# Layer 2, VectorE: the low part of the next batch's first query is made ahead of the statistics of the finished batch

## What is computed

```python
xn = layernorm(x)                          # layer 2's input
a  = layernorm(xn) * g1
q  = l2norm(a @ Wq.T)  * 4                 # 16 heads of 64
k  = l2norm(a @ Wk.T)  * 4;  v = a @ Wv.T  # one head
p  = softmax(causal(q @ k.T))
att = layernorm((p @ v) @ Wout.T) * g2
ffn = (silu(xn @ Wgate.T) * (xn @ Wup.T)) @ Wdown.T
out = x + att + ffn
```

## Time and profile before

| what | value |
|---|---|
| median of 3 runs | 1303.96 us (1302.86 to 1304.91) |
| the profiled execution's own time | 1300.34 us |
| its span, first to last instruction | 1298.5 us |
| mean granted clock of TensorE | 0.964 of full speed |
| busy: PE, DVE, ACT, POOL | 1168.2, 892.5, 669.9, 466.3 us |
| instructions | 27029 |

### The profile page before, as it was taken

How to read it: one execution, slowest core, us unless ns; L and a number is a source line. 1 busy time by engine, 2 the same in 40 slices (tenths; PEclk the granted TensorE clock), 3 DMA queues, 4 the chain that set the end, 5 groups by cost and what they waited for, 6 DMA issues and landing times. The chain is left out here.

```text
span 1298.5 us, 27029 instructions
## 1 busy us (share of the span) xinstructions
PE 1168.2 (90%) x8812; PEld 800.5 (62%) x8812; DVE 892.5 (69%) x2474; ACT 669.9 (52%) x1294; POOL 466.3 (36%) x695
## 2 busy tenths in 40 slices
PE   4999999999999994798199899998999989999896
PEld 2656666565666643798165766657666675766665
DVE  6888888888888856465355766657666576665744
ACT  2667676766767661354064452644526355263540
POOL 4222212222221225553344362634525345263430
PEclk8999999999999995799699999999999999999998
DMA  2310001000100006123000000000000000000000
GB/s 67 100 24 17 18 18 25 17 17 20 23 17 18 23 4 210 45 63 55 8 10 1 9 8 0 16 0 8 8 0 16 0 10 6 0 16 0 9 1 9
DMA packets 34597, 29.78 MB, mean 23 GB/s; under 512 B 5984, under 2 KB 27104, under 8 KB 34528
## 3 DMA queue, kind: packets, MB, share of 16 engines
q1 hardware_dynamic: 32224, 24.22, 6.9%
q0 software_dynamic: 2304, 4.72, 1.7%
HBM read 13.72 MB, written 6.82 MB: 16 GB/s over the span
## 5 line engine op out<-in xcount | busy, mean ns | idle before, releaser
L1272 ACT ACTIVATE arena<-ring_a 128x384 f32<-128x384 f32 (+1 forms) x512 | 252.7, 550 | 138.6 <-PE ring_a L470 138.6
L1417 ACT ACTIVATE arena<-ring_a 128x1024 f32<-128x1024 f32 x128 | 131.6, 1028 | 160.1 <-PE ring_a L470 160.0
L1040 POOL TENSOR_SCALAR_AFFINE_SELECT arena<-arena 128x512 f32<-128x512 f32 x128 | 81.9, 640 | 356.9 <-ACT arena L1272 356.9
L470 PE MATMUL ring_a<-q_max,rows 128*128 128x384 f32 (+1 forms) x512 | 195.4, 385 | 0.9 <-ACT arena L1272 0.5
L1547 DVE CUSTOM_DVE_ANT_0 arena<-pair,arena 128x384 bf16<-128x384 f32 (+1 forms) x271 | 162.3, 614 | 26.4 <-PE pair L470 23.4
L1176 POOL TENSOR_TENSOR q_len<-q_sum,exponents 128x8 f32<-128x8 f32 x64 | 108.1, 1689 | 149.1 <-DVE q_sum L1836 149.1
L470 PE MATMUL pair<-arena,v_aug 128*64 128x512 f32 (+3 forms) x1024 | 150.2, 438 | 4.0 <-ACT arena L1417 3.5
L470 PE MATMUL ring_a<-rows,k_rows 64*128 64x384 f32 (+2 forms) x1152 | 124.8, 339 | 14.8 <-DVE rows L1854 13.8
L470 PE MATMUL ring_a<-arena,v_aug 128*32 128x384 f32 (+1 forms) x1024 | 122.8, 551 | 1.9 <-POOL arena L1040 1.0
L470 PEld LDWEIGHTS pair<-arena,v_aug 128*64 128x64 f32 x1024 | 68.3, 136 | 85.4 <-issue 69.2
L470 PE MATMUL pair<-rows,q_rows 128*128 128x384 f32 (+1 forms) x271 | 110.5, 410 | 3.2 <-DMA rows<-k_rows 2.6
(11 more groups left out here) (251 smaller groups left out, 2196.6 us busy)
## 6 DMA issues: line engine op xcount, KB each, us to landing
rows<-k_rows SPq DMA_DIRECT2D x128, 64.0 KB, 2.0
arena<-in_w SPq DMA_DIRECT2D x2, 2048.0 KB, 14.1
slots_y<-arena SPq DMA_DIRECT2D x40, 64.0 KB, 1.8
x_all<-in_x SPq DMA_DIRECT2D x8, 256.0 KB, 4.0
tokens_x<-xn_all SPq DMA_DIRECT2D x1, 2048.0 KB, 9.6
out<-o_t SPq DMA_DIRECT2D x8, 256.0 KB, 2.3
arena<-tokens_x,tokens_now POOLq DMA_INDIRECT x40, 2.8
wq_sb<-in_wq_t SPq DMA_DIRECT2D x1, 512.0 KB, 4.9
```

Of the source, the lines that this page charges most:

```text
L470: return pe.matmul(out, lhs, rhs, start=start, stop=stop, skip_group_check=True)
L1040: pool.affine_select(out=v, in_=v, compare_op=ALU.is_ge, fill=0.0, base=0, pattern=[[0, HG], [1 if late else -1, P]], channel_multiplier=- ...
L1272: act.activation(probs[:, t % NT, h, 0:many], A.slot(("cols", c))[:, 0:many], ACT.Exp).then_inc(A.free.sem, A.free.add(1))
L1417: act.activation(dst, src, ACT.Exp).then_inc(ring.free.sem, ring.free.add(1))
```

## The change

In the tail of a batch on DVE, the call `first_q_turned(b + 1)` moves from behind `row_stats` of the finished batch to in front of it. No instruction is added or removed; the order of the other engines is the same.

```diff
                 if not last:
                     q_unit(SR, 1, b + 1)
                     k_turned(b + 1)
+                    first_q_turned(b + 1)
                 dve.wait_ge(Z.full.sem, Z.full.at(b, s["e_full"].per))
                 row_stats(s, lambda i: gather[:, i * P:(i + 1) * P], b)
-                if not last:
-                    first_q_turned(b + 1)
                 row_apply(s, 1, lambda i: gather[:, i * P:(i + 1) * P], y1, b).then_inc(s["g_free"].sem, s["g_free"].add(1))
```

## The result

The changed kernel takes 1314.49 us (median of 4 runs, 1312.38 to 1318.13) against 1303.49 us; the ratio is 1.008 with a 95% interval from 1.0061 to 1.0099. It is slower, by 11.0 us or 0.8%. Forecast were 1314.3 us and a range of 1308 to 1318.

A forecast was written before the change was run, and what follows sets the result against it. It took DVE's tail to bound each batch's start, making PE's scores(1) wait. Tail 7.07 us plus clock 3.3 us gave 10.4 us on the profiled 1300.34; with the runs' 3.6 us addition 1314.3 us, range 1308 to 1318.

The forecast's parts named there:

- The gain of scores(0) is waited away: PE's batch start: scores(0) lose their 0.94 us stop, but the stop before scores(1) grows to 2.52 us; value 0.
- The tail sets the time: DVE's tail at each of seven boundaries: statistics and all behind them start 1.01 us later, 7.07 us in sum.
- The wait for ACT: DVE at q_low(0)'s new place: waits about 0.32 us for ACT's high part of q(0), part of the 1.01 us.
- was cover and gives nothing back: DVE between L1461 and L1469: q_low(0)'s vacated place saves nothing; idle time only grows from 1.25 to about 1.95 us.
- The clock: TensorE behind the longer stop before scores(1): clock falls at five of 7 boundaries, 0.65 us each, 3.3 us (0 to 6.0).
- The total of 10.4 us: Whole kernel: 7.07 us of tail plus 3.3 us of clock, giving 1314.3 us, 0.8% slower; forecast's chance 0.56.
- One sign of being wrong: Loop's top on DVE: prediction wrong if `q_sums` starts less than 0.9 us later against the end of `k_turned`.
- The two other signs: Wrong if the batch period stays at 80 us or falls, or the stop before scores(1) stays near 1 us.
- The tail alone: Rival: DVE's tail costs 7.1 us with no fall of TensorE's clock, 1311.0 us; chance 0.29.
- Absorption at the loop's top: Rival: the 0.53 us between `fin` and `q_sums` absorbs part of the shift, leaving 4.4 us, 1308.4; chance 0.06.
- The other side: Rival: PE's first stop counts; ACT's exponentials, 0.51 us earlier, carry through the batch, 3.6 us less, 1300.4; chance 0.05.
- the last rival, no change: Rival: ACT's copy and POOL's root cover each other, so the moved call changes nothing, 1304; chance 0.04.

The follow-up runs named there:

- run 5: Kernel before, q_low(0) at its old place, finished batch's last two steps (times g2, plus the rest) moved from DVE to POOL mid next batch: 1300.16 us.
- run 6: Changed kernel, q_low(0) early, finished batch's last two steps (times g2, plus the rest) moved from DVE to POOL mid next batch: 1297.17 us.
- run 4: Changed kernel with two separate queue instructions (wait for k.T's bank, count for q.T's) moved from in front of q_low(0) to behind it: 1312.63 us.
- run 1: Changed kernel plus one more 128x512 subtraction, output unused, on DVE behind the statistics: 1316.8 us.
- Run 3: Changed kernel with PE kept at work in the stop before scores(1) by 12 more matmuls whose result is overwritten: 1309.17 us.
- run 2: Kernel before, q_low(0) at its old place, plus one more 128x512 subtraction, output unused, on DVE in front of the statistics: 1308.38 us.
- run 7: Changed kernel with the finished batch's last two steps given to POOL at once, ahead of its first length of the next batch: 1320.8 us.
- run 8: Changed kernel with the last two steps on POOL mid next batch, and the queue instructions behind q_low(0) instead of in front: 1296.91 us.

## Why the prediction was right, and where it was not

- **The gain of scores(0) is waited away: right.** The first stop went, the second grew from 1.01 to 2.40 us (2.52 forecast). Runs 5 and 6 show the same gain coming through when the second stop isn't DVE's.
- **The tail sets the time: right, its size wrong.** The term was 7 x 1.01 = 7.07 us; it measured 7 x 0.77 = 5.4. Three parts were off. The wait for ACT was 0.52 instead of 0.32 us, because a wait and a count stand as instructions of their own in front of q_low(0); run 4 takes that out. The subtraction itself put the statistics off by 0.61 us (817.61 to 818.22) and not by its 0.69, as the next instruction starts before it ends. And the sentence that failed is that what q_low(0) leaves behind "was cover and gives nothing back". It was cover for DVE, but POOL's L1009 was held up by it: 0.60 us beside it, 0.23 without, 0.47 with a substitute in run 1. DVE's idle time before L1469 went to 1.59 us, not to 1.95. The price stood in the trace ahead: L1009 takes 0.23 us elsewhere in phase C and 0.60 only at this place. I read POOL's root as one block and didn't compare its durations. The Trainium skill, "SBUF — State Buffer", section "SBUF: two separate sides", says that a DVE instruction with two SBUF inputs and a GpSimd instruction that reads SBUF exclude each other for the whole instruction. The trace agrees for this place: q_low reads two SBUF tensors, and POOL's instruction ended 0.09 us behind DVE's subtraction in the kernel before and in run 1. The other way round it doesn't: in run 6 q_low(1) started 0.22 us behind POOL's L1176, which took 1.64 us, and still ran its usual 0.69.
- **The clock: right that it falls, its size too small.** Forecast 5 x 0.65 = 3.3 us, measured 6 x 0.78 = 4.7 in the profiled execution. The five was a choice, so that it came near is in part luck. Run 3 shows that it is the clock. By the Trainium skill, "TensorE: Matmul & The Clock Gate", section "HAM oscillation — how this bites in real kernels", the stops here are too short for a fall; this kernel doesn't keep to that: stops of 2.19 to 2.43 us were followed by a fall six times in seven, and the last batch's stop of 1.90 us in one of the two traces.
- **The total of 10.4 us against 11.0 measured (10.1 from the periods) is closer than its terms, and that is luck.** 1.7 us too much for the tail and 1.4 too little for the clock offset each other.
- **One sign of being wrong came true.** `q_sums` were to start at least 0.9 us later against `k_turned`; they start 0.73 later. Likewise q_low(0) starts 0.24 us behind ACT's high part, not 0.04, and the period without a fall is 80.77 us, not 81.0. By the prediction's own words it is wrong there, and what failed is the size of the tail's shift. The two other signs stayed away: the period rose, and the stop before scores(1) grew.
- **The rivals.** The tail alone, forecast as 7.1 us more, is what run 3 is, with 5.2. Absorption at the loop's top is out: q_sums stayed 0.53 us behind `fin` and moved with it (824.66 - 824.13). The other side is real in its premise, ACT's exponentials start 0.65 us earlier against `k_turned` (4.17 to 3.52), but it decides nothing while scores(1) wait for the tail: the kernel got slower, not faster. That puts out the last rival, no change, too.

## What to carry to other kernels

An instruction that stands in an engine's wait is free only there; before moving it forward, ask who is behind it in the same queue and whether that chain, not the consumer that gains, ends the next wait. If the consumer's gain runs into a second wait, shorten that one first: the same move cost 11.0 us with the long tail and gained 3.0 us with the short one. And where a stop of TensorE grows, count a fall of its clock as part of the price: in this kernel it came behind 1.45 us at two of seven boundaries and behind 2.4 us at six of seven.

## What the runs showed of the hardware

- The granted clock fell from 2.4 to 1.2 GHz behind stops of PE of 2.2 to 2.4 us in six of seven cases (changed kernel), of 2.0 to 2.2 in five of seven (run 4), of 1.45 to 1.48 us in two of seven (run 2), and at a boundary whose stops were about 1 us in none (before, runs 5, 6 and 8). The same stop of 1.90 us in the last batch was followed by a fall in six of the ten traces. One fall cost 0.69 to 0.94 us behind scores(1), and 1.5 to 1.75 us in run 7.
- POOL's 128x4 instruction took 0.23 us alone and 0.60 or 0.47 us beside a 128x512 subtraction of DVE, ending 0.09 us behind it both times. POOL's 128x8 root took 1.64 us where DVE's subtraction started behind it and 2.01 where it started just ahead; DVE's subtraction took 0.68 or 0.69 us either way.
- Two DVE instructions of 0.69 us with no wait between them started 0.60 us apart (run 2). A wait and a count as separate instructions ahead of a DVE instruction cost 0.20 us (run 4), behind it nothing measurable.
